# One projection moved ahead of the first V product in a fused linear-attention and gated-MLP kernel

## The reference

```python
xn = _layernorm(x, axis=-1)
# attention: 16 query heads, 4 key/value heads, head size 128
q, k, v = xn @ wq.T, xn @ wk.T, xn @ wv.T          # split into heads
q, k = _rope(q), _rope(k)                          # k, v repeated for the 4 query heads of a group
def step(kv, inp):                                 # over chunks of the sequence, per head
    qi, ki, vi = inp
    scores  = einsum('bhid,bhjd->bhij', qi, ki) * diag[None]         # decayed scores inside a chunk
    o_intra = einsum('bhij,bhje->bhie', scores, vi)
    o_inter = einsum('bhid,bhde->bhie', qi * q_dec, kv)              # what earlier chunks left
    kv = blk * kv + einsum('bhjd,bhje->bhde', ki * k_dec, vi)
    return kv, o_intra + o_inter
s = o @ wo.T
g = silu(ffn(xn))                                  # fp8-rounded weights, silu(gate) * up, then down
return x + s * g
```

## Time and profile before

| | |
|---|---|
| median of three runs | 925.86 us (925.5 to 926.18) |
| the profiled execution, its own time | 924.73 us |
| span of its instructions | 922.9 us |
| TensorE busy | 899.3 us (97%), 4128 matmuls |
| VectorE busy | 627.0 us (68%) |
| ScalarE busy | 421.7 us (46%) |
| GpSimd busy | 362.2 us (39%) |
| mean granted TensorE clock, of full speed | 0.998 |
| DMA over the span | 150 GB/s |

### The profile page before, as it was taken

The page is one execution under the profiler, slowest core; times in us unless marked ns, Lnnn a source line. Parts: engine busy times, 40 slices in busy tenths (PEclk is TensorE's granted clock), DMA queues, the critical chain, the costliest instruction groups (busy, mean ns, idle before and its releaser), DMA issues.

```text
span 922.9 us, 12461 instructions
## 1 busy us (share of the span) xinstructions
PE 899.3 (97%) x4128; PEld 738.6 (80%) x4128; DVE 627.0 (68%) x915; ACT 421.7 (46%) x709; POOL 362.2 (39%) x267
## 2 busy tenths in 40 slices
PE   5999999999999999999999999999999999999996
PEld 4888888888888878888888888878888878878776
DVE  7778653586553346666687766776866678779686
ACT  3643533443432555444455344464554454543531
POOL 1011112121122565535535545455455364554541
PEclk9999999999999999999999999999999999999999
DMA  6792213469650542331443504333423145356352
GB/s 209 226 368 91 103 46 125 174 241 326 251 205 7 199 153 110 137 121 61 145 143 119 199 23 160 135 117 136 158 81 136 38 167 205 105 181 227 115 182 81
DMA packets 51403, 138.55 MB, mean 150 GB/s; under 512 B 4256, under 2 KB 25888, under 8 KB 45984
## 3 DMA queue, kind: packets, MB, share of 16 engines
q1 hardware_dynamic: 51360, 138.00, 42.5%
HBM read 96.04 MB, written 41.94 MB: 150 GB/s over the span
## 4 chain that ended last, share of the span: by engine, by line
PE 43%; issue 30%; POOL 19%; DVE 4%; ACT 1%; DMA 1%; POOLq 0%; SPq 0%; DVEq 0%; ACTq 0%
PE bank L1210 43%; POOL d_r L1168 10%; POOL rot L1177 9%; PE bank L1257 1%; DVE d_sb L1001 1%; DMA stage<-in_x_nat 1%; DMA tail_sb<-mlp_gate 1%; DVE q_r L994 0%; DVE d_sb L1046 0%; DVE rot L987 0%; ACT d_r L682 0%; ACT gout L538 0%; DVE rot L988 0%; ACT rot L662 0%; ACT st_r L671 0%
## 5 line engine op out<-in xcount | busy, mean ns | idle before, releaser
L1210 PE MATMUL bank<-xn,aw 128*128 128x512 f32 x960 | 228.6, 389 | 0.0
L1177 POOL TENSOR_TENSOR rot<-rot 128x512 f32<-128x512 f32 x80 | 127.8, 1597 | 236.6 <-DVE rot L988 236.6
L1210 PEld LDWEIGHTS bank<-xn,aw 128*128 128x128 f32 x960 | 179.2, 188 | 36.6
L1168 POOL TENSOR_TENSOR d_r<-d_sb,d_r 128x512 fp32r<-128x512 f32 x128 | 166.6, 1329 | 51.9 <-ACT d_r L682 51.9
L1210 PE MATMUL bank<-o_r,ow 128*128 128x512 f32 (+1 forms) x816 | 186.4, 379 | 0.0
L1210 PE MATMUL bank<-xn,gu_w 128*128 128x512 f32 x768 | 179.9, 389 | 0.0
L1210 PEld LDWEIGHTS bank<-xn,gu_w 128*128 128x128 f32 x768 | 144.2, 188 | 30.1
L1210 PEld LDWEIGHTS bank<-o_r,ow 128*128 128x128 f32 x816 | 145.7, 188 | 27.5
L682 ACT CAST d_r<-d_sb 128x512 fp32r<-128x512 f32 x128 | 78.9, 621 | 100.4 <-DVE d_sb L1046 67.1
L987 DVE TENSOR_TENSOR rot<-bank,rope 128x512 f32<-128x512 f32 x80 | 55.2, 690 | 98.0 <-ACT rot L662 97.8
L661 ACT COPY rot<-bank 64x512 f32<-64x512 f32 x80 | 46.7, 584 | 145.9 <-PE bank L1210 145.4
(11 more groups left out here) (75 smaller groups left out, 946.1 us busy)
## 6 DMA issues: line engine op xcount, KB each, us to landing
xn<-xn_split SPq DMA_DIRECT2D x15, 2048.0 KB, 7.8
v_decayed<-vd_split SPq DMA_DIRECT2D x32, 512.0 KB, 3.4
vd_r<-v_decayed SPq DMA_DIRECT2D x16, 1024.0 KB, 6.9
v_r<-v_split SPq DMA_DIRECT2D x16, 512.0 KB, 5.8
wst<-in_mlp_w SPq DMA_DIRECT2D x10, 768.0 KB, 5.3
xn_split<-xn SPq DMA_DIRECT2D x3, 2048.0 KB, 10.8
stage<-in_attn_w SPq DMA_DIRECT2D x4, 1280.0 KB, 6.1
stage<-in_x_nat SPq DMA_DIRECT2D x16, 256.0 KB, 4.7
```

The lines of the kernel that those rows point to most:

```text
L1168: pool.tensor_tensor(d_r[:, slot(e), 1, :], d_sb[:, slot(e), :], d_r[:, slot(e), 0, :].bitcast(F32), ALU.subtract).then_inc(d_lo, 1)
L1177: pool.tensor_tensor(rot1[:, r % RRING, :], rot1[:, r % RRING, :], rot2[:, r % RRING, :], ALU.add).then_inc(qk_sum, 1)
L1210: last = pe.matmul(dst, a, b, start=start and x == 0, stop=stop and x == len(pairs) - 1)
```

## The change

`LAG` and the loop over t are gone from `step` on TensorE, and the same calls are written out. P0 moves from behind V2 to behind S4, ahead of V0; V0 now stands ahead of S5, and V1 behind it. On ScalarE and VectorE the split of weight tile 0 in an edge step moves from behind block 3 to ahead of it. GpSimd's and SyncE's orders stay. Line numbers below line 35 are one lower after the change.

```diff
-LAG = 3
 ...
 # ScalarE
             def step(n, g, b, start=False, edge=False, final=False, last=False):
+                if edge:
+                    aw_split_hi(g + 1, 0)
                 for t in range(HEAD, NBL):
                     decayed_round(n, SC + t)
-                    if edge and t == HEAD:
-                        aw_split_hi(g + 1, 0)
 ...
 # VectorE
+                if edge:
+                    aw_split_lo(g + 1, 0)
                 for t in range(HEAD, NBL):
                     decay_block(n, t)
-                    if edge and t == HEAD:
-                        aw_split_lo(g + 1, 0)
 ...
 # TensorE
             def step(n, g, b, start=False, edge=False, final=False, last=False):
                 g_edge = g + 1 if edge else None
-                for t in range(HEAD, NBL + LAG):
-                    if t < NBL:
-                        scores(n, t)
-
-                    if t == NBL and not last:
-                        project(n + 1, 0, g_edge)
-                    if t >= LAG:
-                        times_v(n, t - LAG)
+                scores(n, HEAD)
+                scores(n, HEAD + 1)
+                if not last:
+                    project(n + 1, 0, g_edge)
+                times_v(n, 0)
+                scores(n, HEAD + 2)
+                for t in range(1, NBL):
+                    times_v(n, t)
```

## The result

The changed kernel takes 932.54 us (median of four runs, 932.24 to 933.15), the kernel before 926.02 us beside it (925.5 to 927.0). The ratio is 1.007, with a 95% interval of 1.0053 to 1.0087: 6.5 us slower. The forecast was 930.6 us, in a range of 927.0 to 933.0.

A forecast was written before the change was run, and what follows sets the result against it. TensorE, busy 97% of the span, was taken to bound the kernel, so reordering wins only its waits. Ordinary steps +1.1, edge steps +3.6 and last step 0 gave +4.7 on 925.86: 930.6 us, range 927.0 to 933.0.

The forecast's parts named there:

- V0's wait is gained: Ordinary step, TensorE: S4 and P0 ahead of V0 cover its wait for GpSimd's subtraction, gaining 0.32 us.
- Block 5 is late at V5: Ordinary step: block 5 reaches V5 at 8.61 behind S3, due 8.23; wait 0.38, plus 0.12 behind it.
- The four links: S5 to VectorE's decay, ScalarE's cast, GpSimd's start, then the product V5: 0.97, 0.80, 0.70, 1.35, together 3.82 us.
- The sum over ordinary steps: Twelve ordinary steps, S3 to P1: seven lose 0.13 each, five 0.03 each; +1.1 us, +-0.2 a step.
- The edge steps: Three edge steps: P0 waits 0.94 for weight tile 0's split, P1 at 10.47 behind S3; +1.2 each, +3.6 us.
- The third rival: Edge steps: the split waits for a whole GpSimd subtraction, up to 1.94; 2.2 each, 933.6 us; chance 0.07.
- The second wait of V5: V5's wait for the first output tile (`o_lo`), over at 8.4 behind S3, 0.1 to 0.2 before 8.61; not deciding.
- The last step: Step without P0: the swap of V0 and S4 fills V0's wait, GpSimd's row returns it; 0, between -0.3 and +0.1.
- The transposes of an edge step: Behind P1 in an edge step: they wait already, 5.80 behind P1; the wait stays, neither growing nor hiding the 1.2.
- Block 5 in time: Rival: S5 to V5 takes at most 3.3, so V5 doesn't wait; -2.9, 923.0 us; chance 0.07.
- The edge wait hidden: Rival: weight tile 0 is split before S4 ends, edge steps cost 0.1; +1.4, 927.3 us; chance 0.13.
- The forecast, 928.2 to 932.6: Listed fourth among the rivals: the summed time, by +-0.2 a step on the ordinary steps; chance 0.73.

The follow-up runs named there:

- the order with all scores first: Against the kernel before, TensorE alone changed: S3, S4, S5, then V0, V1, V2, then P0, V3, V4, V5; ratio 0.9964, and 0.9969 when measured again.

## Why the prediction was right, and where a size was off

**V0's wait is gained: right.** V0 is at 4.11 behind S3 in the ordinary steps, as summed, and has no wait in any of the fifteen steps with a P0.

**Block 5 is late at V5: right in each link.** The four links were forecast as 0.97, 0.80, 0.70 and 1.35 and measured so. V5 was forecast at 8.61 and is at 8.60; P1 at 9.41 and is at 9.40 to 9.42 in the looped steps. In the two steps outside a loop, n = 0 and 12, P1 is at 9.31, since V5 comes at 8.54.

**The sum over ordinary steps**, forecast as +1.1, measured +1.6 in the first profile of the change, +1.25 in the second, and +1.17 with only these steps changed. That it came so close is in part luck, for two errors cancel. I had summed at P1, and there the twelve steps are only 0.65 later in the first profile (112.76 against 112.11). The seven steps lose 0.13 each, as summed; but the five others (n = 0, 1, 4, 12, 13), which had more of V0's wait to lose and for which I had taken +0.03 each, come out 0.27 earlier together. The rest came behind P1, where I had summed nothing: 0.03 in each step for catching up with the weights between P1 and the transposes, and 0.43 in n = 12, although I had written that nothing behind P1 has less slack than the transposes. A wait of 0.17 ahead of `inter` at the end of n = 5, in the first profile, is not of the change's making: the order with all scores first shows it too.

In n = 12 VectorE has the output weights' split and the final sums in the same step, the rotation of the key comes 0.65 later, and the second block of the next scores waits 0.60 for `q_r` instead of 0.17. From S0 to `inter` of that step it is 3.64 to 3.70 in the six profiles with the whole of P0 ahead of V2 there, and 3.21 or 3.22 in the six others. That the wait comes from P0's new place is shown by this; the way over VectorE is read from the rows and not tested by a run of its own.

**The edge steps: the mechanism right, the term mis-sized.** Forecast +1.2 each, 3.6; measured 1.66, 1.94 and 1.85, together 5.45, and 5.34 with the edge steps alone changed. P0 was to start at 2.31 behind S3, and started at 2.70, 3.02 and 2.97. The mis-sized term is what an edge step waits. It was short by three parts, two at P0 and one at P1:

- The split took 1.33 to 1.35, and I had taken 0.94 from a row of the old place. ScalarE's cast began 0.67 behind S3 and VectorE's split 1.32, both as forecast. This is 0.4 in each step. The Trainium skill (SBUF — State Buffer, Who interferes with whom) says that a VectorE instruction with two SBUF inputs and a GpSimd instruction that reads SBUF block each other fully, by order of issue. The rows here agree: 1.35 beside GpSimd's row and 0.68 with GpSimd idle, and GpSimd's three subtractions in that stretch took 4.24 instead of 3 x 1.26 = 3.78. I had weighed the rule against one row, 0.94, and taken it for the split's length in this company; n = 3 has 1.12 in the same trace. A split ends 0.55 behind the end of the subtraction that it meets, and moving it changes which one that is and how much is left of it. The rows of before give the size: in n = 7 GpSimd's subtraction ran until 2.11 behind S3, so a split begun at 1.31 would end at 2.66 and P0 start at 2.72 (measured: 2.64 to 2.67, and 2.70 where no other delay came on top). The row is 601.16 to 602.45, with S3 at 600.34. The third rival (1.94) was the upper end of this by the prediction's own sum; by the rule of the rows it is 1.26 + 0.55 = 1.81.
- In the two looped edge steps P0 started 0.35 and 0.32 behind the end of the split and not 0.06. Three more waits stood behind the one for the weights. With that wait last it was 0.06, and P1 came 0.25 earlier.
- P1 waits too. Ahead of the prediction I had written that it has no wait. That holds in an ordinary step only; in an edge step it waits for weight tile 1, whose split stands behind the first two output tiles. VectorE begins it 10.74 behind S3 (613.80), and P1 could have started at 10.38 + 0.80 = 11.18. It cost 0.3 in each edge step; with the split between blocks 4 and 5 it was gone. The shorter wait at the transposes gave 0.2 of it back.

**The second wait of V5** was called close and not deciding. That holds, by 0.02 and not by 0.1 to 0.2: the tile is done at 8.45, where 8.4 was summed, and the 0.13 from VectorE to TensorE was not counted.

**The last step: right.** V5 is at 7.25 behind S3 before and after.

**The transposes of an edge step** were to keep their wait. They lost 0.2 of it (5.58 behind P1 for 5.80), because P1 was held longer than V5. TensorE's busy time was called unchanged and is 1.5 us more (900.8 for 899.3).

**The rivals.** Block 5 in time: out, the links are what they were. The edge wait hidden: out. The forecast, 928.2 to 932.6, held the time, but by 0.06 only (its own +-0.2 on each of twelve steps would make the upper end 933.0, not 932.6). The sum, +4.7, was short by 1.8, nearly all of it from the edge steps. So the direction and the mechanism were right, and the size was about three quarters of the measured one.

## What to carry to other kernels

A wait at the first product of a chain needs enough other work ahead of it, and not all that can be found. Here two blocks of scores (1.4 us) covered V0's wait of 0.2 to 0.3, while the whole projection on top (2.7 us) ran into the room of two later chains. Before work is moved ahead of a product, measure the distance from each producer to its consumer behind it: here S5 to V5 needed 3.8 and V2 to V5 needed 2.4, and the change left less than that at both, so that mending one gained only 0.04 a step. Where the moved work is fed by another engine in a few steps only, those steps have to be summed by themselves, with every wait of the moved work and of what follows it.

## What the runs showed that I had not expected

- Dividing a chain of 12 accumulating matmuls in two, with six matmuls into other banks between the halves, cost nothing that the timeline shows: P1 at 8.93, the pace.
